# A lightning-attention block on one core: values as a fourth group of seven products, keys and values turned in squares of 32 by way of DRAM

## The reference

```python
x  = L0_attn_hidden_states                      # (4, 512, 512) f32
xn = layernorm(x)
qkv = silu(einsum('bnf,of->bno', xn, w_qkv))    # 16 heads of q, k, v, 128 each
# causal linear attention with a decay per head, in blocks, state kv (128 x 128):
#   o = (q * q_decay) @ kv + ((q @ k.T) * diag_decay) @ v
#   kv = block_decay * kv + (k * k_decay).T @ v
out = norm_w * out * rsqrt(mean(out * out) + eps)
s = einsum('bno,fo->bnf', sigmoid(xn @ w_gate.T) * out, w_out)
# a router over the same xn: softmax over 64 experts, top 8
scores = softmax(xn @ router_weight.T + router_bias); topk_w, topk_idx = top_k(scores, 8)
ffn = xn * sum(topk_w) + sum(topk_w * expert_bias[topk_idx])
result = x + s * silu(ffn)
```

## Time and profile before

| | |
|---|---|
| median of three runs | 1111.96 us (1111.66 to 1113.95) |
| the profiled execution | 1112.18 us, its span 1110.4 us |
| TensorE busy | 1086.9 us (98%) |
| VectorE, ScalarE, GpSimd busy | 593.0, 513.8, 564.7 us |
| granted TensorE clock | 0.997 of full speed |
| DMA | 73.11 MB, 19.8% of the 16 engines' time |

### The profile page before, as it was taken

The page is one execution under the profiler, slowest core; times in us unless marked ns, Lnnn a source line. Parts: engine busy times, 40 slices in busy tenths (PEclk is TensorE's granted clock), DMA queues, the critical chain, the costliest instruction groups (busy, mean ns, idle before and its releaser), DMA issues.

```text
span 1110.4 us, 17104 instructions
## 1 busy us (share of the span) xinstructions
PE 1086.9 (98%) x6552; PEld 962.5 (87%) x6552; DVE 593.0 (53%) x1078; ACT 513.8 (46%) x819; POOL 564.7 (51%) x448
## 2 busy tenths in 40 slices
PE   5999999999999999999999999999999999999996
PEld 5988888898988989888898888989888898988985
DVE  6845454535445353567548645344554545456656
ACT  5745262443526344462544625334352533536245
POOL 4646464454546445363547736446463544527135
PEclk9999999999999999999999999999999999999998
DMA  7262111101111110112814211011111101110122
GB/s 253 79 244 95 39 39 57 39 20 53 43 39 39 47 50 20 38 50 84 308 53 133 76 40 39 22 55 39 39 41 55 39 20 57 39 39 20 39 76 76
DMA packets 28080, 73.11 MB, mean 66 GB/s; under 512 B 3040, under 2 KB 3168, under 8 KB 28000
## 3 DMA queue, kind: packets, MB, share of 16 engines
q1 hardware_dynamic: 28000, 72.02, 19.8%
HBM read 59.43 MB, written 12.58 MB: 65 GB/s over the span
## 4 chain that ended last, share of the span: by engine, by line
PE 94%; DVE 1%; POOL 1%; ACT 1%; issue 1%; DMA 0%; SPq 0%; DVEq 0%; ACTq 0%; POOLq 0%
PE st_ps L474 12%; PE st_ps L476 12%; PE st_ps L475 12%; PE v_ps L562 5%; PE v_ps L564 5%; PE v_ps L563 5%; PE out_ps L633 5%; PE score_ps L588 5%; PE out_ps L634 5%; PE out_ps L635 5%; PE head_ps L616 5%; PE tk_ps L599 4%; PE head_ps L619 4%; PE tk_ps L580 2%; PE st_ps L463 1%; PE st_ps L465 1%
## 5 line engine op out<-in xcount | busy, mean ns | idle before, releaser
L474 PE MATMUL st_ps<-xt_hi,w_hi 128*128 128x512 f32 x616 | 253.0, 411 | 0.2 <-DVE q_t L1598 0.2
L476 PE MATMUL st_ps<-xt_hi,w_lo 128*128 128x512 f32 x616 | 241.8, 393 | 0.0
L475 PE MATMUL st_ps<-xt_lo,w_hi 128*128 128x512 f32 x616 | 240.5, 390 | 0.0
L1353 POOL TENSOR_TENSOR w_lo<-land_a,w_hi 128x768 fp32r<-128x768 f32 x44 | 81.2, 1846 | 230.6 <-ACT w_hi L950 230.6
L1683 DVE TENSOR_TENSOR acc<-acc,out_ps 128x512 f32<-128x512 f32 x120 | 82.5, 688 | 213.1 <-PE out_ps L635 212.9
L1371 POOL TENSOR_TENSOR w_lo<-land_a,w_hi 128x1024 fp32r<-128x1024 f32 x44 | 109.6, 2492 | 94.8 <-ACT w_hi L955 94.8
L476 PEld LDWEIGHTS st_ps<-xt_hi,w_lo 128*128 128x128 f32 x616 | 115.6, 188 | 25.7
L562 PE MATMUL v_ps<-wv_hi,xt_hi 128*128 128x256 f32 (+1 forms) x472 | 136.0, 288 | 0.0
L564 PE MATMUL v_ps<-wv_hi,xt_lo 128*128 128x256 f32 (+1 forms) x472 | 134.6, 285 | 0.0
L563 PE MATMUL v_ps<-wv_lo,xt_hi 128*128 128x256 f32 (+1 forms) x472 | 134.5, 285 | 0.0
L475 PEld LDWEIGHTS st_ps<-xt_lo,w_hi 128*128 128x128 f32 x616 | 116.4, 189 | 20.1
(11 more groups left out here) (311 smaller groups left out, 2217.2 us busy)
## 6 DMA issues: line engine op xcount, KB each, us to landing
land_a<-wgrp_dram SPq DMA_DIRECT2D x48, 512.0 KB, 3.6
land_b<-wv_dram SPq DMA_DIRECT2D x16, 512.0 KB, 3.7
land_b<-wo_dram SPq DMA_DIRECT2D x16, 512.0 KB, 3.5
xt_hi<-spill_hi SPq DMA_DIRECT2D x16, 256.0 KB, 5.1
xt_lo<-spill_lo SPq DMA_DIRECT2D x16, 256.0 KB, 5.7
out_dram<-acc SPq DMA_DIRECT2D x16, 256.0 KB, 2.0
spill_hi<-gate_hi SPq DMA_DIRECT2D x11, 256.0 KB, 2.0
spill_lo<-gate_lo SPq DMA_DIRECT2D x11, 256.0 KB, 2.5
```

Source lines behind the costliest of these rows:

```text
L474: pe.matmul(ps[:, :], w_h2, x_h2, start=first and k == 0, stop=False, skip_group_check=True)
L475: pe.matmul(ps[:, :], w_h2, x_l2, start=False, stop=False, skip_group_check=True)
L476: end = pe.matmul(ps[:, :], w_l2, x_h2, start=False, stop=last and k == 1, skip_group_check=True)
```

## The change

- The values become a fourth group `VAL` of seven products in steps 1 to 15, between QK0 and QK1. Step 0 keeps `v_fill`. VAL's weights land in `land_b` from step 2 on. `v_fill`, `take_v` and the values' weight split are gone from the later steps.
- Values and keys then stand with features on the partitions. VectorE turns each 32 x 32 square in place of a full turn (`square_keys`, `square_values`). The squares are stored to DRAM (`k_squares`, `v_squares`) and loaded back with the squares swapped (`swap_keys`, `values_out`, `values_back`): four transfers for each way back, one for 32 partitions each, whose contiguous pieces are 32 floats. TensorE turns no keys after step 0, and `take_k_rows` scales the keys in place when they are back.
- The router's scores are made by themselves in steps 6 and 14 (`router_scores`), 96 matmuls of 64 columns, all into the bank `v_ps`.
- The order of all engines' steps is written anew around this. `kv_products` of head 0 moves later in QK1; the output tiles stand among VAL's and QK1's products; the weights' high parts of VAL are the first work of ScalarE in a step. In the closing step the bias products all use one bank.

```diff
-QK0, QK1, GATE = range(3)
+QK0, QK1, GATE, VAL = range(4)
+TURN = (0, 2, 3, 1)
...
+    k_squares = nc.dram_tensor("k_squares", (P, 2 * (NCH - 1) * HD), F32, kind="Internal").ap()
+    v_squares = nc.dram_tensor("v_squares", (2, P, 2 * SEQ), F32, kind="Internal").ap()
...
+        v_t = sb("v_t", [P, 2, 2, SEQ])
...
-            return 3 * ss + g
+            return 3 + 4 * (ss - 1) + TURN[g] if ss else g
+        def landed(ss, g):
+            return 8 + 3 * (ss - 2) + g if ss > 1 else group(ss, g) + 1
+        def landing(ss, g):
+            return land_b[:, :].rearrange("p (a k o) -> p a k o", a=4, k=2) if g == VAL and ss > 1 else land_a
...
+        def k_turned(h, b):
+            if h == 0:
+                return state[:, b, :, :].rearrange("p c d -> p (c d)")
+            return v_t[:, 0, :, :].rearrange("p b s -> p (b s)")[:, b * (NCH - 1) * HD:(b + 1) * (NCH - 1) * HD]
+        def v_block(i):
+            first = state[:, :, :, :].rearrange("p b c d -> p (b c d)")[:, 0:SEQ]
+            return ((0, 0, first), (1, 1, v_t[:, 0, 0, :]), (1, 0, v_t[:, 1, 1, :]), (0, 1, v_t[:, 1, 0, :]))[i]
...
+            def load_group(pair, ss, g):
+                n = group(ss, g)
+                if g == VAL and ss > 1:
+                    sp.wait_ge(wo_l, ss)
+                    sp.dma_start(land_b[:, :], wgrp[4 * pair + g]).then_inc(w_in_b, 16)
+                else:
+                    sp.wait_ge(w_l, 2 * (n - (g == QK1 and ss > 1)))
+                    sp.dma_start(land_a[:, :, :, :].rearrange("p a k o -> p (a k o)"), wgrp[4 * pair + g]).then_inc(w_in, 16)
+            def load_out(pair, ss):
+                if ss == 0:
+                elif ss == 1:
+                    sp.wait_ge(wo_l, 1)
+                else:
+                    sp.wait_ge(w_l, 2 * group(ss, VAL) + 2)
+            def swap_keys(ss, h):
+                at = 2 * (ss - 1) + h
+                src = state[:, :, :, :].rearrange("p b c d -> p (b c d)") if h == 0 else v_t[:, 0, :, :].rearrange("p b s -> p (b s)")
+                sp.wait_ge(k_squared, 2 * (at + 1))
+                if at:
+                    sp.wait_ge(k_in, 64 * at)
+                sp.dma_start(k_squares, src[:, 0:2 * (NCH - 1) * HD]).then_inc(k_out, 16)
+                sp.wait_ge(k_out, 16 * (at + 1))
+                sp.wait_ge(kv_full, unit(ss, h, 0))
+                rows = k_squares.rearrange("(i a) (m j e) -> j a m i e", i=4, j=4, e=32)
+                for j in range(4):
+                    sp.dma_start(k_row[32 * j:32 * j + 32, :, :, :].rearrange("a b c (i e) -> a (b c) i e", e=32),
+                                 rows[j]).then_inc(k_in, 16)
+            def values_out(ss, i):
+                h, b, src = v_block(i)
+                sp.wait_ge(v_squared, 4 * (ss - 1) + i + 1)
+                if ss > 1 and i < 2:
+                    sp.wait_ge(v_in[b], 64 * (ss - 1))
+                sp.dma_start(v_squares[b][:, h * SEQ:(h + 1) * SEQ], src).then_inc(v_out[b], 16)
+            def values_back(ss, b):
+                sp.wait_ge(v_out[b], 32 * ss)
+                sp.wait_ge(head_full, 4 * ss)
+                rows = v_squares[b].rearrange("(i a) (m j e) -> j a m i e", i=4, j=4, e=32)
+                for j in range(4):
+                    sp.dma_start(v_row[32 * j:32 * j + 32, b, :, :, :].rearrange("a h c (i e) -> a (h c) i e", e=32),
+                                 rows[j]).then_inc(v_in[b], 16)
...
+                swap_keys(ss, 0)
+                values_out(ss, 0)
+                load_group(pair, ss, GATE)
...
                 load_out(pair, ss)
+                values_out(ss, 1)
+                values_out(ss, 2)
+                values_back(ss, 0)
+                values_out(ss, 3)
+                values_back(ss, 1)
+                if ss < LAST:
+                    load_group(after, ss + 1, QK0)
...
+                swap_keys(ss, 1)
...
+                load_group(after, ss + 1, VAL)
...
+                load_group(after, ss + 1, QK1)
...
+            def router_scores(b):
+                if b == 0:
+                    pe.wait_ge(ffn_const_l, 2)
+                for t in range(b * NCH, (b + 1) * NCH):
+                    c = t % NCH
+                    dst = v_ps[:, t * NEXP:(t + 1) * NEXP]
+                    for k in range(KC):
+                        blk = ((B11, B12), (B21, B22))[k // 2][b]
+                        x_h2, x_l2 = (xt[:, blk, k % 2, c * P:(c + 1) * P] for xt in (xt_hi, xt_lo))
+                        pe.matmul(dst, x_h2, router_hi[:, k, :], start=k == 0, stop=False, skip_group_check=True)
+                        pe.matmul(dst, x_h2, router_lo[:, k, :], start=False, stop=False, skip_group_check=True)
+                        end = pe.matmul(dst, x_l2, router_hi[:, k, :], start=False, stop=k == KC - 1, skip_group_check=True)
+                end.then_inc(router_full, 1)
...
+                p4(ss, QK0)
+                p3(ss, QK0)
+                scores(ss, 0, 0)
+                p1(ss, VAL)
+                scores(ss, 0, 1)
+                p2(ss, VAL)
+                output_tile(before, 0)
...
+                p6(ss, VAL)
+                output_tile(before, 1)
+                p5(ss, VAL)
+                p7(ss, VAL)
                 if has_router(ss):
+                    router_scores(0)
+                output_tile(before, 2)
...
+                p4(ss, VAL)
+                output_tile(before, 3)
+                if has_router(ss):
+                    router_scores(1)
+                p3(ss, VAL)
+                p1(ss, QK1)
...
+                p2(ss, QK1)
+                output_tile(before, 4)
+                p6(ss, QK1)
+                output_tile(before, 5)
...
+                p5(ss, QK1)
+                p7(ss, QK1)
+                kv_products(ss, 0, 0)
...
+                output_tile(before, 6)
...
+                p4(ss, QK1)
+                output_tile(before, 7)
...
+                kv_products(ss, 0, 1)
...
+                p3(ss, QK1)
...
             def take_k_rows(ss, odd, h, b):
                 u = unit(ss, h, b)
-                act.wait_ge(turned, u + 1)
-                if u >= 2:
-                    act.wait_ge(kv_full, u - 1)
-                act.activation(k_row[:, b, :, :].rearrange("p c d -> p (c d)"), tk_ps[:, 0:(NCH - 1) * HD], ACT.Copy,
+                dst = k_row[:, b, :, :].rearrange("p c d -> p (c d)")
+                if ss == 0:
+                    act.wait_ge(turned, u + 1)
+                    if u >= 2:
+                        act.wait_ge(kv_full, u - 1)
+                else:
+                    act.wait_ge(k_in, 64 * (2 * (ss - 1) + h + 1))
+                act.activation(dst, dst if ss else tk_ps[:, 0:(NCH - 1) * HD], ACT.Copy,
                                scale=pair_cols[:, odd, KEY + h:KEY + h + 1]).then_inc(k_row_set, 1)
...
+                raw_hi(ss, VAL)
+                if ss > 1:
+                    act_c12(before, GATE)
                 take_square(before, 0, 1)
...
+            def square_keys(ss, h, b):
+                dve.wait_ge(acted, 4 * group(ss, h) + (A_C22 if b else A_C21))
+                if h == 0:
+                    dve.wait_ge(head_full, 4 * ss)
+                else:
+                    dve.wait_ge(v_out[0], 32 * ss)
+                    dve.wait_ge(v_out[1], 32 * ss)
+                dve.transpose(k_turned(h, b), k_t[:, b, 0:(NCH - 1) * CH]).then_inc(k_squared, 1)
+            def square_values(ss, i):
+                h, b, dst = v_block(i)
+                dve.wait_ge(acted, 4 * group(ss, VAL) + i + 1)
+                if i == 0:
+                    dve.wait_ge(k_out, 32 * (ss - 1) + 16)
+                else:
+                    dve.wait_ge(v_squared, 4 * (ss - 1) + i)
+                dve.transpose(dst, v_t[:, h, b, :]).then_inc(v_squared, 1)
```

More of the change, by code:

```diff
@@ L398, in _ @@
-            load_group(PAIRS - 1, group(ss, GATE), GATE)
-            load_out(PAIRS - 1, ss)
-            sp.wait_ge(prod, prods(group(ss, GATE)))
+            load_group(1, 1, VAL)
+            load_group(1, 1, QK1)
+            for ss in range(1, 2 * PAIRS):
+                step(ss % PAIRS, ss)
+            sp.wait_ge(prod, prods(FINAL))
             for t in range(TILES):
                 if t == 6:
-                    sp.wait_ge(w_l, 2 * group(ss + 1, QK0))
+                    sp.wait_ge(w_l, 2 * FINAL + 2)
@@ L467, in direct_block, with block_product @@
                     end.then_inc(made, 1)
-            def block_product(ps, buf, wblk, xblk, first, last):
+            def block_product(ps, ss, g, wblk, xblk, first, last):
+                buf = group(ss, g) % 2
                 for k in range(2):
@@ L581, in turn_and_score, with scores @@
                 last.then_inc(turned, 1)
+            def scores(ss, h, b):
+                u, n = unit(ss, h, b), group(ss, h)
+                if ss:
+                    pe.wait_ge(acted, 4 * n + (A_C21 if b == 0 else A_C12))
                 if u:
@@ L1094, in step @@
                 gate_high(before, 1, 0)
```

(39 more changed lines are left out.)

697 lines of the change are left out of this document (291 added, 406 removed).

## The result

The changed kernel takes 1121.95 us (median of 8 runs, 1118.6 to 1127.11) against 1111.97 us before (8 runs, 1111.3 to 1113.95): ratio 1.0092, 95% interval 1.0074 to 1.0111. The profiled execution took 1123.63 us, its span is 1121.8.

The account below looks back on a forecast made before the run. TensorE's own work was taken as the bound (busy 98%): 1112.2 - 32.5 (TensorE's floor) + 9.5 (step 1) + 3 (closing step, short waits) = 1092.2, forecast 1092 us. Own range 1079 to 1108; with rivals 1078 to 1165.

Parts of the forecast that it names:

- TensorE's floor: TensorE's own work over all steps falls by 32.5 us: 24.7 from products, 19.3 from key turns, less 11.5 for router.
- The router: Steps 6 and 14: 96 matmuls of 64 columns standing alone, 0.106 us each, add 11.5 us in all (-1.5 to 14).
- None becomes the bound: VectorE (41 us of a 62 us step), GpSimd (38) and ScalarE gain work, but only TensorE sets the end.
- 3 (0 to 8): Allowance of 3 us, ends 0 and 8, for the closing step's bias products in one bank and for short waits.
- The way through DRAM: Values and keys return in 128-byte pieces at 13 ns each; the last values take 15.2 us against 17.2, margin 2.
- rival (b): SyncE is held 1.3 us per way-back issue in place of 0.45: 1.4 us a step, 1113 us; chance 0.10.
- (a): Small pieces on the way back cost 26 ns: 4.6 us of wait a step, 1161 us; chance 0.29.
- Step 1: Late weight loads and ScalarE's order delay head 1's square, the second scores and output tile 0: net 9.5 us, once.
- The estimate of 24 ns a piece: Price of a piece on the way back, from the skill's strided copy as a transpose; would give about 1146 us.

Follow-up runs that it names:

- x2: Changed kernel with the 96 router matmuls issued twelve at a time behind eight products, in place of two runs of 48: 1113.9 us, ratio 1.0005.
- x1: Changed kernel with only 8 of the 96 router matmuls issued in each of steps 6 and 14: 1096.53 us, ratio 0.9850.
- x3: Changed kernel with each router matmul moving 256 columns in place of 64, runs of 48 unbroken: 1115.81 us, ratio 1.0023.
- x4: Changed kernel with VectorE's router parts 3, 4, 5 and 7 placed earlier, only VectorE's order changed: 1118.47 us, ratio 1.0060.
- x7: Changed kernel with the second batch's values brought back from DRAM twice, the second time after the first landed: 1210.65 us, ratio 1.0876.
- x8: Changed kernel with router matmuls twelve at a time, VectorE's router parts earlier, step 1's order and load changed, block loads merged: 1101.16 us, ratio 0.9893.
- x12: x10 with GpSimd's low part of the sums of VAL's weights moved behind the last square's adding in step 1: 1093.47 us, ratio 0.9827.
- x9: x8 without the merged block loads, and with step 0's output weights split before step 1: 1098.45 us, ratio 0.9873.
- x10: x9 with the router's weights stationary and 512 tokens moving, 24 matmuls and 8 transposes a router step: 1088.88 us, ratio 0.9791.

## Why the prediction was wrong, by its own steps

Two terms of the sum failed, the router's and the one for short waits. They make 13.5 and 15 us of the error of 31.5 in the profiled run.

**TensorE's floor.** Right for the ordinary steps: -2.93 us each, where 1.9 + 1.29 = 3.2 was worked out. The nine fell short by 2 us.

**The router.** This is the first step that failed, "11.5 (ends -1.5 and 14)", which measured 24.9 (+12.0 and +10.3 in the table, and 1.29 each for the turns gained there): "96 matmuls of 64 columns stand alone", at 0.106 us by the row of 16 one-column matmuls. The price was nearly right (0.112). What was assumed without a word was that the clock of the rows holds in a run of 48. It doesn't: x2 gets 9.7 us back by the ratio (11.5 in the steps of its trace) with the same 96 matmuls at full clock; x1 and x3 show that the fall comes from these matmuls and from their being short. Sixteen of them in a row could not show it, and the price's upper end, 0.120 a matmul, was no end at all: at half clock it is 0.2135, and the products behind pay as well. (The lower end was slightly off too: the line through 256 and 320 columns gives 0.041, not 0.038.) Of these 13.5 us 2 are price.

**"None becomes the bound".** True of the sums (VectorE 43.5 of 62.3 us in an ordinary step) and wrong where it mattered. This is the second step that failed, and the larger. I priced VectorE by its total and didn't place the router's parts and the closing work in steps 7, 8 and 15 among the added evictions and turns; "3 (0 to 8)" for the closing step and short waits measured 18: 9.3 in step 7, 5.7 in step 8, 3.3 in step 15. x4 got 3.6 us of it back by VectorE's order alone. The 2.5 to 3 us in step 7 for the second half's blocks I put down to B12, whose load was moved behind P1 of GATE though nothing in step 7 reads it any more. This is argued from the two orders and the DMA's rate, not tried. The four waits of step 8 (4.6 us idle) stand much the same in every run but x7; no run touched them, and their cause stays open.

**The way through DRAM.** Right, and the closest call: no kv product waits in the changed kernel. The 215,040 pieces of 128 bytes take 13 ns each in the trace (median), the value taken from the middle of 5.4 and 22; neither bound was tight, so that it is met to the nanosecond is luck. SyncE is held 0.65 to 0.69 us by such an issue, not 0.45 (four in 2.7 us): rival (b)'s direction, at a quarter of its size. It used 0.9 us of the margin, and 1.3 us are left in an ordinary step (median) where 2 were worked out. Rivals (a) and (b) didn't come. But most of the larger mends ran into it: TensorE waits for the values in step 9 of x1, x3 and x8 to x12, 0.9 to 2.3 us idle.

**Step 1.** The dates were right: 3.9 us of wait before head 1's output as forecast, the second scores at 108.0 (107.1), the output tile at 112.9 (112); +7.0 for the part against +6.3. What filled the time between them was not. Idle time in step 1 rose by 5.2 us (7.1 against 1.8), not by 9.5, and the granted clock, for which the forecast had no term, was at half for 10.2 us; before it had no such stretch there:

```profile
93.70:97.10 3.40, 3.40 (x12) 2.82 (x11) 0.69 (x1) 3.37 (x7) 3.24 (x4) 0.50 0.00 0
107.30:114.10 6.80, 5.89 (x17) 4.62 (x18) 1.85 (x3) 3.56 (x6) 5.50 (x4) 0.50 0.37 58
```

ScalarE and GpSimd set the dates, so I read it that slower matmuls took the place of waiting; no run took the two apart.

**The rules weighed.** The Trainium skill (DMA: Bandwidth & Descriptors, Specifications) gives 512 bytes as the least for full rate, as below it an engine reads and modifies before it writes. The trace agrees with the first half: 13 ns for 128 bytes beside 84 for 2048, so 2.5 times as much a byte. That anything is read and modified, no row shows, and the price stayed within the chain's margin. The estimate of 24 ns a piece, from the Trainium skill (VectorE: DVE Perf Modes, The three transpose paths), was nearly twice the 13 measured.

The sign was wrong because steps 6, 7, 8, 14 and 15 cost 28.8 us more than the sum had, against a gain of 20. With work put in another order alone the change gives most of what was worked out: x9 is 6 us above the forecast of 1092, and x10, whose router is also a cheaper one, 3 below it.

## What to carry to other kernels

When cheap matmuls are moved out from behind wide ones, price the run they then form, not the single one: look whether any row shows as many in a row at full clock, and spread them or turn operands so that the long side moves. Work that is hidden in an average step must be placed anew in the steps with extra work, engine by engine. And a chain with a margin of 1 or 2 us is a debt: each later gain on TensorE is paid out only until it is used up.

## What was not expected of the hardware

A run of 48 matmuls of 64 columns, each behind its own weight load and without a gap, brings the granted clock from 2.4 to 1.2 GHz (0.112 to 0.2135 us a matmul); 256 columns in the same run don't, nor do twelve of 64 at a time.

VectorE's instructions that read two operands from SBUF are held while GpSimd works. All low parts of the gates, before and changed (min, median and max in ns):

```profile
L1674 DVE TENSOR_TENSOR gate_lo<-gated,gate_hi x60: 678/684/1271, 93.5 to 1046.6; 128x512 fp32r<-128x512 f32 x60
```

```profile
L1725 DVE TENSOR_TENSOR gate_lo<-gated,gate_hi x60: 675/692/2885, 100.0 to 1055.1; 128x512 fp32r<-128x512 f32 x60
```

In the changed kernel those that meet no GpSimd work take 0.69 us (median of 28), those that lie mostly beside it 2.39 (median of 19). The other form with both operands in SBUF, `q_t<-q_t,decay`, goes from 0.55 to 0.92 (up to 2.08), while sums with one operand in PSUM and the turns stay at 0.69 and 0.57 to 0.71 beside GpSimd. Two operands are not the whole of it: the copy of `pair_cols`, 128x8 from SBUF to SBUF, takes 0.16 us free and 1.37 beside GpSimd (14 of 16). The Trainium skill (SBUF — State Buffer, SBUF: two separate sides) has it so: a VectorE operation with two SBUF inputs and a GpSimd operation that reads SBUF take a shared pair of ports in turn, whole instructions long. x12 agrees: 4.10 to 1.91 us. The change made this dearer: the gates' low parts take 68.2 us in place of 47.1. I put that down to the added GpSimd work (four sums and a longer rest per step) and to both engines' new orders.
